# Expert blocks of a mixture-of-experts layer: the seven down products of a block issued in one series instead of one by one

## The reference, cut to what matters

```python
up = jax.nn.silu(hn @ qgroup(w1[e]).T) * (hn @ qgroup(w3[e]).T)   # 256 -> 896
moe = moe + rw[:, e:e + 1] * (up @ qgroup(w2[e]).T)               # 896 -> 256
```

## Time and profile before

| | before |
|---|---|
| time, median of 3 runs | 1216.11 us (1215.24 to 1216.46) |
| the profiled execution: its time | 1217.11 us |
| its span, first to last instruction | 1215.4 us |
| mean granted TensorE clock | 0.912 |
| PE, PEld busy | 983.3 us (81%), 734.5 us (60%) |
| DVE, ACT, POOL busy | 959.9 (79%), 744.8 (61%), 600.7 us (49%) |
| L2158 (up products) on the chain that ended last | 16% of the span |
| L2168 (down products) on that chain | 11% of the span |

### The profile page before, as it was taken

The page is one execution under the profiler, slowest core; times in us unless marked ns, Lnnn a source line. Parts: engine busy times, 40 slices in busy tenths (PEclk is TensorE's granted clock), DMA queues, the critical chain, the costliest instruction groups (busy, mean ns, idle before and its releaser), DMA issues.

```text
span 1215.4 us, 24888 instructions
## 1 busy us (share of the span) xinstructions
PE 983.3 (81%) x7366; PEld 734.5 (60%) x7367; DVE 959.9 (79%) x2172; ACT 744.8 (61%) x1885; POOL 600.7 (49%) x639
## 2 busy tenths in 40 slices
PE   0495786537998899868999999963999999999990
PEld 0342443325777777745666666743888888888880
DVE  6859999988888888758999988746777777777673
ACT  4864343406888888826667676532666666666663
POOL 2859777752444444413476667633243434343323
PEclk9597988767999988979999999985999999999995
DMA  5850010031333333143222122120122212222214
GB/s 195 348 204 0 1 35 17 17 112 59 122 127 125 129 128 118 56 132 150 100 70 70 42 64 71 61 68 14 37 39 37 37 39 37 39 37 39 34 30 147
DMA packets 53493, 96.77 MB, mean 80 GB/s; under 512 B 9840, under 2 KB 41584, under 8 KB 52928
## 3 DMA queue, kind: packets, MB, share of 16 engines
q1 hardware_dynamic: 45328, 83.35, 19.8%
q0 software_dynamic: 8112, 12.78, 6.0%
HBM read 66.37 MB, written 29.74 MB: 79 GB/s over the span
## 4 chain that ended last, share of the span: by engine, by line
PE 44%; DVE 36%; issue 9%; POOL 4%; ACT 3%; DMA 3%; DVEq 0%; ACTq 0%; POOLq 0%; SPq 0%
PE banks L2158 16%; PE banks L2168 11%; DVE mix_sums L685 4%; DVE peak L1186 2%; DVE whole_stat L241 2%; DVE whole_stat L240 2%; DVE probs L1189 2%; DVE carry L672 2%; DVE carry L675 2%; PE banks L1452 2%; PE banks L1430 1%; PE banks L1475 1%; PE banks L1467 1%; PE banks L924 1%; DVE top L655 1%
## 5 line engine op out<-in xcount | busy, mean ns | idle before, releaser
L2252 DVE SCALAR_TENSOR_TENSOR expert_gate<-banks,expert_steps,expert_chunk 128x128 f32<-128x128 f32 x546 | 166.4, 347 | 98.1 <-ACT expert_chunk L2214 96.1
L2158 PE MATMUL banks<-expert_parts,levels 128*128 128x128 bf16 x3276 | 229.5, 221 | 7.1 <-issue 5.5
L2158 PEld LDWEIGHTS banks<-expert_parts,levels 128*128 x3276 | 203.3, 99 | 47.8 <-issue 20.1
L2168 PE MATMUL banks<-down,up 128*128 x546 | 176.2, 406 | 0.0
L2214 ACT COPY expert_chunk<-banks 128x256 f32<-128x256 f32 x273 | 101.6, 372 | 105.9 <-PE banks L2158 105.9
L2323 POOL DMA_INDIRECT summed_d<-expert_y,expert_target x39 | 62.5, 1602 | 180.7 <-ACT expert_y L2224 177.8
L488 PE MATMUL banks<-x_turned,w_rkv 128*128 128x512 f32 (+1 forms) x192 | 104.0, 704 | 40.0 <-DVE weight L666 35.5
L2218 ACT ACTIVATE silu<-expert_gate,expert_steps 128x128 f32<-128x128 f32 x273 | 110.7, 405 | 15.9 <-DVE expert_gate L2252 15.8
L1151 POOL TENSOR_TENSOR whole<-whole_level,whole_stat 128x896 bf16<-128x896 f32 x32 | 53.2, 1684 | 101.5 <-DVE whole_level L1226 101.5
L488 PEld LDWEIGHTS banks<-x_turned,w_rkv 128*128 128x128 f32 x192 | 42.5, 227 | 98.6 <-issue 93.4
L2259 DVE SCALAR_TENSOR_TENSOR up<-expert_gate,expert_steps,silu 128x128 f32<-128x128 f32 x273 | 94.8, 347 | 8.2 <-ACT silu L2218 8.2
(11 more groups left out here) (265 smaller groups left out, 2457.2 us busy)
## 6 DMA issues: line engine op xcount, KB each, us to landing
whole_raw<-in_weight_jobs SPq DMA_DIRECT2D x16, 896.0 KB, 5.3
levels_d<-whole_t SPq DMA_DIRECT2D x16, 448.0 KB, 2.8
levels<-levels_d SPq DMA_DIRECT2D x16, 448.0 KB, 3.7
raw<-in_weight_jobs SPq DMA_DIRECT2D x6, 896.0 KB, 4.7
numbers_d<-turned SPq DMA_DIRECT2D x6, 896.0 KB, 6.6
down<-in_weight_jobs SPq DMA_DIRECT2D x5, 896.0 KB, 8.3
normed_d<-normed_parts SPq DMA_DIRECT2D x16, 192.0 KB, 1.8
attend_w<-numbers_d SPq DMA_DIRECT2D x3, 896.0 KB, 6.5
```

What stands on the lines that cost most here:

```text
L2158: last = pe.matmul(banks[:, at, (m * DC + c) * ROWS:(m * DC + c + 1) * ROWS], levels[:, bass.ds(expert * (2 * JOB) + (m * JOB + (f * DC + ...
L2168: last = pe.matmul(banks[:, Y + j, 0:D], up[j][:, f, :], down[:, bass.ds(expert * JOB + f * D, D)], start=(f == 0), stop=(f == FC - 1))
L2252: last = dve.scalar_tensor_tensor(out=gate[slot(j, f)][:, m, :], in0=halves(at)[:, m, 1, :], scalar=steps[j][:, m, 1, f:f + 1], in1=chunk[ ...
```

## The change

Five edits, all in `experts_stage`:

1. On PE the seven down products of block n - 1 stand together, ahead of up product 3 of block n (`MID` = 3), instead of one behind each up product.
2. The turning of block n + 1 stands behind that series, in the same place in the row of up products as before (between f = 2 and f = 3).
3. On ACT `take_rows` for block n + 1 stands directly ahead of `first_chunk` 3 (before: behind `first_chunk` 4 and `soften` 3), with `soften` 2 moved ahead of it; and `take_y` of block n - 1 stands behind `first_chunk` 3 (before: at the end of the step, behind `soften` 6).
4. The expert's number is loaded once per block, behind the turning, into one of two registers that are kept; the step reads the registers.
5. The wait for `parts_ready` stands at the first up product.

The banks, the buffers, DVE's and POOL's code are the same.

```diff
+    MID = 3
+    DOWN_RUNS = {MID: range(0, FC)}
...
-        def expert_of(n):
-            return pe.value_load(k.block_expert[0:1, bass.ds(n, 1)], min_val=0, max_val=E - 1)
+        expert_held = [pe.alloc_register(f"expert_{j}") for j in range(2)]
+
+        def load_expert(j, n):
+            pe.reg_load(expert_held[j], k.block_expert[0:1, bass.ds(n, 1)])
+
+        def expert_of(j):
+            return pe.snap(expert_held[j], min_val=0, max_val=E - 1)
...
         def step(j, n, i, prev, more):
-            expert = expert_of(n)
-            last_expert = expert_of(n - 1) if prev else None
-            pe.wait_ge(parts_ready, n + 1)
+            expert = expert_of(j)
+            last_expert = expert_of(1 - j) if prev else None
             for f in range(FC):
+                if prev and f in DOWN_RUNS:
+                    for d in DOWN_RUNS[f]:
+                        down_product(1 - j, n - 1, d, last_expert)
+                if more and f == MID:
+                    turn(1 - j, n + 1, i + 1 if prev else 0)
+                    load_expert(1 - j, n + 1)
+                if f == 0:
+                    pe.wait_ge(parts_ready, n + 1)
                 up_product(j, n, f, expert)
-                if prev:
-                    down_product(1 - j, n - 1, f, last_expert)
-                if more and f == 2:
-                    turn(1 - j, n + 1, i + 1 if prev else 0)
...
             for f in range(FC):
+                if f == MID:
+                    soften(j, n, f - 1)
+                    if more:
+                        take_rows(1 - j, n + 1)
                 first_chunk(j, n, f)
-                if f:
+                if f and f != MID:
                     soften(j, n, f - 1)
-                if more and f == 4:
-                    take_rows(1 - j, n + 1)
+                if prev and f == MID:
+                    take_y(1 - j, n - 1)
             soften(j, n, FC - 1)
-            if prev:
-                take_y(1 - j, n - 1)
```

More of the change, by code:

```diff
@@ L2198, in tensor @@
         pe.wait_ge(k.expert_loads, 16 * (WHOLES + E - LATE))
+        load_expert(0, 0)
         turn(0, 0, 0)
         in_steps(step, pe)
-        expert = expert_of(BLOCKS - 1)
+        expert = expert_of(0)
         for f in range(FC):
```

## The result

The changed kernel takes 1222.85 us (median of five runs, 1220.38 to 1224.14); the kernel before took 1216.11 in the same rounds. The ratio is 1.005, its 95% interval 1.0037 to 1.0064: 4.5 to 7.8 us slower. The forecast was 1215.7 us in a range of 1210.5 to 1221.0, with "no change" as the likeliest outcome. The time lies above the range, and the loss, though only half a per cent, is clear of the noise.

The account below looks back on a forecast made before the run. It took TensorE's instruction stream to bound the kernel, with DVE's rhythm deciding after the change. +2.5 (pairs) - 0.5 (front) - 2.4 (last scatter) = -0.4 us, so 1216.11 goes to 1215.7 us, range 1210.5 to 1221.

Parts of the forecast that it names:

- DVE's rhythm: DVE's chunks 3 to 6 behind a turning: 0.91 us apart, making PE stall 1.18 and 0.24 us at the next block.
- The first rival: Shorter DVE rhythm or earlier chunk 3 copy, so a smaller stall: 1209.7 us at 0.80 a chunk, 1190 without stall; chance 0.14.
- The front of block 1, -0.5 us: Ahead of block 1 PE idles 0.52 us behind two loads; that goes, saving between 0 and 0.5 us.
- PE's own work of 16.2 us a pair: PE's instructions alone: 8.09 us a block, 16.18 a pair instead of 17.47, if nothing else decided.
- the gain of 23 us and the pause: PE's shorter work over 18 pairs gains 23 us; the stall for banks costs 18 x 1.42 = 26; net +2.5.
- the 0.14 from DVE to PE: Wait on the bank, from DVE's end to PE's start: 0.14 us; at nothing or twice that, 2.5 us less or more.
- no cost of the load: The one load behind the turning costs 0, at most 0.30 us a block, 11 us; rival that it shows: chance 0.10.
- clock 1.00 from 880 to 1160 us: TensorE's clock stays 1.00 despite pauses of 1.2 us a pair; rival that it falls: 1259 us, chance 0.03.
- the target didn't hold ACT: POOL's target is ready 0.6 us before `take_y` wants it; rival that it holds up ACT: 9 us, 1224.7, chance 0.07.
- The end: The last scatter starts 1.30 us after `take_y` instead of 3.71, no longer waiting for the scatter before: -2.4 us.
- a quarter of the load's 11 us: Within the rival that each load behind the turning shows (11 us, 1226.7; chance 0.10), a quarter price giving 1219.4 us.
- 0.61 us inside the pair: Excess at block borders, 0.10 us at one and 0.51 at the loop's jump, gone with the change and counted in the pair.

Follow-up runs that it names:

- e9: The changed kernel with VectorE's program for the stage written out block by block, the other engines keeping their loop: 1218.72 us.
- e1: The changed kernel with a fifth PSUM bank for the up products, both down sums sharing one bank: 1193.85 us.
- e3: The kernel before with only the expert's number held in registers, one load a block at the step's end: 1206.43 us.
- e13: The changed kernel with ScalarE's old order (e7) plus a fifth bank for the up products: 1240.28 us.
- e11: The changed kernel with the down products in two series, three ahead of the turning and four ahead of up product 6: 1209.36 us.
- e8: The changed kernel with both the fifth bank for the up products and seven gate buffers: 1189.34 us.
- e12: The changed kernel with three loads of the expert's number behind each turning instead of one, each with a reader: 1223.36 us.
- e2: The changed kernel with seven gate buffers instead of two: 1210.6 us.
- e7: The changed kernel with ScalarE's order of before (rows copied behind the fifth chunk's silu, y taken at the step's end): 1263.8 us.

## Why the prediction was wrong

**The step that failed is DVE's rhythm, "chunk 4 at 2.53, chunk 5 at 3.44, chunk 6 at 4.35: 0.91 each".** The 0.38 us between `multiply` and the next gate came from the earlier trace rows, block 0, which is straight code; 17 of the pairs run in the loop, where it is 0.46. Chunk 5's gate comes 0.18 later than forecast (0.02 of it from chunk 3 at 1.64 instead of 1.62), so the first up product starts at 1.64 + 2 x 0.99 + 0.61 + 0.14 = 4.37 behind the turning, which is what the trace has (992.41 to 996.78), instead of 4.19. Chunk 6's comes 0.26 late, so the half ends 0.27 late. With 0.04 more in the short half, a pair is 17.92 and not 17.61: 17 x 0.31 = 5.3 us, where the stage missed its forecast by 5.4. The first rival looked at just this number, asked only whether it could be shorter in the loop, and found "the same instructions in the loop"; the arithmetic is the same, but the wait that ends last stands on another instruction. e9 shows it.

That 5.3 and 5.4 agree so well is in part luck, since two other terms were off in opposite directions. The sum counted 18 pairs at 17.47 us before, but the last one, which has no jump, took 17.06 (8.54 and 8.52), so the change costs 0.4 us more there than forecast. And the front gave 0.3 us more:

**The front of block 1, -0.5 us, came by another way.** I put the idle 0.52 of the earlier trace rows down to loads, since DVE was done. With the loads gone DVE's chain reaches further: in block 0 ACT's copy of the rows stands behind a silu and starts 1.88 us behind its turning (848.03 to 849.91) instead of 0.53, chunk 5 ends at 853.48, and PE idles 0.79. With the fifth bank (e1) that half is 9.83 us instead of 10.92, so the bank costs 1.09 there too, which the forecast left out. Yet from the first turning to block 1's first up product it is 11.17 us (842.56 to 853.73), before 11.98 (840.72 to 852.70). In block 0 the granted clock rises from 0.50 to 1.00, and it did so earlier behind the first turning, at 5 us instead of 8. The windows, first of before, then of after (the column behind the five busy times is the clock):

```profile
848.00:849.00 1.00, 1.00 (x18) 1.00 (x16) 0.25 (x2) 0.53 (x2) 0.39 (x3) 0.83 0.00 0
```
```profile
847.00:848.00 1.00, 1.00 (x13) 1.00 (x12) 0.47 (x3) 0.68 (x2) 1.00 (x2) 0.57 0.00 0
```

Over the fourteen profiles this moment lies between 4 and 8 us behind the first turning (4 to 5 in e3 and e13, 8 in e11 and e9, though in e9 only VectorE's program differs from after's), and it goes with no edit. How much of the 0.81 us it made isn't separated, so the gain at the front can't be put down to the loads.

**Right were:** the mechanism (a bank's wait turns the series' gain into a pause, e1); the series of 3.08 us; PE's own work of 16.2 us a pair (e8: 16.21); that the gain of 23 us and the pause cancel but for a few us; the 0.14 from DVE to PE; no cost of the load (e12); the last scatter 1.28 us behind its sum, forecast 1.30; clock 1.00 from 880 to 1160 us; `take_y` 1.49 behind the turning, so the target didn't hold ACT.

**The end came as forecast.** The last scatter starts 1.28 us behind its sum instead of 3.71: -2.4. From the last turning to the last scatter it is 20.00 us before and 15.74 after, but 1.8 of these 4.3 us are only moved: the four down products that used to stand behind the turning stand ahead of it now, and from block 1's first up product to block 2's turning it takes 5.22 us now (853.73 to 858.95) and took 3.48 (852.70 to 856.18).

**One figure of the prediction doesn't follow:** a quarter of the load's 11 us on top of 1215.7 is 1218.5, not 1219.4. It touches one price of a rival and at most the upper end of the range, not the sum.

**What I didn't see** is that the change held two edits of opposite sign. The held number alone gives 10 us to before (e3). Against e3 the series with its ScalarE order costs 16.7 us of stage. The change loses, and the better kernel was one of its own parts. The prediction priced the held number as 0.61 us inside the pair and called most of it the jump's; it was right that it goes, but the row could as well have been read as "one edit alone brings 17 x 0.61 us".

## What to carry to other kernels

Before a change makes an engine's rhythm decide, read that rhythm from rows inside the loop: of two waits on one operation one stood on an instruction of its own, in the loop another than in straight code, and it cost 0.07 to 0.08 us where it was the last to be met and nothing where it was early. When work is gathered into a series, count for each buffer or bank how much work lies between its release and its next use; a bank more was worth 29 us here, and moving four of the seven products behind the turning 13. Put loads of registers where products are already queued: three in the middle of a block cost nothing (e12), one at a step's end, ahead of the jump, nothing that shows (e3), two behind the jump half a us (before). And when a change holds several edits, time each of them alone.

## What the runs showed of the hardware

- Of two waits ahead of one VectorE operation, one is an instruction of the sequencer: 0.04 us in the loop, where it also computes a value, 0.02 in straight code. Met last, it adds 0.08 us to the hand-over from `multiply` (0.46 against 0.38) and 0.07 to that from ACT's copy (0.09 against 0.02, with a constant); met early, it adds nothing (0.26 in e2).
- A load of a register on TensorE's queue takes 0.30 us. Three of them behind six transposes cost 0.0 us a block; two at each block's start cost 0.6 to 0.7 us a pair.
- With TensorE pausing 1.19 us every 17.9, the granted clock stayed 1.00; with 1.70 us every 19.1 it fell to 0.50 behind ten of the 18 pauses, and 24 matmuls took 2.62 us instead of 1.51 (e7); with pauses of 0.4 us twice a block it stayed 1.00 (e13).
- Between executions of kernels with the same instructions up to there but for one register load, the stage began at 838.9 to 843.3 us; its length agreed to 0.1 us wherever the work was the same (349.6 and 349.5; 354.6, 354.7 and 354.7). In block 0 the granted clock rose from 0.50 to 1.00, 4 to 8 us behind the first turning.
